# Softmax totals of a causal attention: four steps of probabilities instead of two summed before one product with ones

## The reference, cut to what matters

```
scores = jnp.einsum('bhqd,bhkd->bhqk', q, k) / jnp.sqrt(hd)
scores = jnp.where(causal, scores, -inf)
attn = jax.nn.softmax(scores, axis=-1)
y = jnp.einsum('bhqk,bhkd->bhqd', attn, v)
```

## Time and profile before

| | us |
|---|---|
| median of three runs | 2745.73 |
| lowest and highest | 2738.48, 2749.93 |
| the profiled execution | 2743.38 |
| its span on the core | 2741.5 |
| PE busy | 2482.9 |
| DVE busy | 1624.8 |
| POOL busy | 1320.2 |
| ACT busy | 1056.7 |

### The profile page before, as it was taken

The page is one execution under the profiler, slowest core; times in us unless marked ns, Lnnn a source line. Parts: engine busy times, 40 slices in busy tenths (PEclk is TensorE's granted clock), DMA queues, the critical chain, the costliest instruction groups (busy, mean ns, idle before and its releaser), DMA issues. The chain is left out here.

```text
span 2741.5 us, 40031 instructions
## 1 busy us (share of the span) xinstructions
PE 2482.9 (91%) x13407; PEld 1621.5 (59%) x13407; DVE 1624.8 (59%) x3253; ACT 1056.7 (39%) x1885; POOL 1320.2 (48%) x827
## 2 busy tenths in 40 slices
PE   6789999998758999999999999999779875999997
PEld 4667677777534444444444444444258764888885
DVE  5544555110458777777777777777136554767666
ACT  3521001111331555555555555555411111444443
POOL 3452442000432767676767676667624453333332
PEclk8999999999886999999999999999989987999998
DMA  7356655312743515151515151511186755878875
GB/s 263 108 155 198 176 168 170 95 39 61 262 134 80 133 39 133 37 134 37 135 37 136 36 134 38 121 47 48 31 274 215 168 117 179 304 280 302 296 283 195
DMA packets 231902, 397.20 MB, mean 145 GB/s; under 512 B 44540, under 2 KB 95292, under 8 KB 231620
## 3 DMA queue, kind: packets, MB, share of 16 engines
q1 hardware_dynamic: 204340, 319.62, 40.2%
q0 software_dynamic: 17152, 50.38, 5.3%
q10 hardware_dynamic: 10256, 25.21, 2.9%
HBM read 299.22 MB, written 103.76 MB: 147 GB/s over the span
## 5 line engine op out<-in xcount | busy, mean ns | idle before, releaser
L1184 ACT ACTIVATE t_prob<-t_scores_psum 128x512 f32<-128x512 f32 (+3 forms) x1280 | 610.5, 538 | 440.0 <-PE t_scores_psum L1076 241.8
L1306 POOL TENSOR_TENSOR t_two<-t_prob 128x1024 f32<-128x1024 f32 (+1 forms) x321 | 687.8, 2165 | 164.7 <-ACT t_prob L1184 110.9
L1212 DVE TENSOR_REDUCE t_part<-t_seen_psum 128x1 f32<-128x512 f32 x768 | 479.2, 682 | 141.0 <-PE t_seen_psum L1049 137.0
L1049 PE MATMUL t_seen_psum<-t_k_stack,t_q_stack 97*128 97x512 f32 (+3 forms) x1283 | 522.0, 419 | 39.6 <-DVE t_q_stack L1200 22.5
L1072 PE MATMUL t_scores_psum<-t_q_stack,t_k_stack 98*128 98x512 f32 (+3 forms) x1280 | 502.8, 404 | 5.3 <-ACT t_prob L1184 3.9
L1072 PEld LDWEIGHTS t_scores_psum<-t_q_stack,t_k_stack 98*128 98x128 f32 x1280 | 241.9, 190 | 301.5 <-ACT t_prob L1184 165.5
L1049 PEld LDWEIGHTS t_seen_psum<-t_k_stack,t_q_stack 97*128 97x128 f32 x1283 | 256.8, 201 | 90.8 <-DVE t_part L1212 36.8
L1218 DVE CUSTOM_DVE_ANT_0 t_seen_psum<-t_seen_psum,t_causal 128x128 f32<-128x128 f32 (+3 forms) x515 | 250.6, 504 | 100.9 <-PE t_seen_psum L1049 89.8
L1090 PE MATMUL t_y_acc_psum<-t_prob,t_v 128*32 128x512 f32 (+3 forms) x2576 | 301.4, 540 | 0.0
L1591 PE MATMUL z_acc_psum<-z_e_hi,z_x_hi 128*128 128x512 f32 x576 | 228.1, 396 | 0.0
L1593 PE MATMUL z_acc_psum<-z_e_hi,z_x_lo 128*128 128x512 f32 x576 | 224.9, 390 | 0.0
(11 more groups left out here) (234 smaller groups left out, 3892.7 us busy)
## 6 DMA issues: line engine op xcount, KB each, us to landing
z_raw<-in_expert_w SPq DMA_DIRECT2D x80, 512.0 KB, 6.8
z_spare<-in_expert_w SPq DMA_DIRECT2D x72, 512.0 KB, 7.1
f_w_raw<-in_wmod SPq DMA_DIRECT2D x8, 2048.0 KB, 10.1
t_q_stack<-scratch_q_hi SPq DMA_DIRECT2D x64, 256.0 KB, 5.1
t_k_stack<-scratch_k_hi SPq DMA_DIRECT2D x64, 256.0 KB, 5.0
f_w_raw<-in_w_attn SPq DMA_DIRECT2D x24, 512.0 KB, 7.0
t_inverse<-scratch_inverse SPq DMA_DIRECT2D x132, 64.0 KB, 2.0
t_y<-scratch_a_y SPq DMA_DIRECT2D x33, 256.0 KB, 4.5
```

The source lines that it names most:

```text
L1049: nc.tensor.matmul(seen[:, n % BANKS, 0:width], q_stack[par][0:SEEN, h, t0:t0 + P], k_stack[par][0:SEEN, h, c * CH:c * CH + width], start= ...
L1184: nc.scalar.activation(prob[:, step % RING, h, c0:CH], scores[:, score_bank(step, h), c0:CH], ACT.Exp, scale=1.0 / math.sqrt(D)).then_inc( ...
L1212: nc.vector.tensor_reduce(dst, seen[:, n % BANKS], AX.X, ALU.max).then_inc(seen_free, 1)
L1306: nc.gpsimd.tensor_tensor(two[:, pair % 2, heads, c0:CH], a, b, ALU.add).then_inc(two_ready, 1)
```

## The change

The sum in `two` takes four steps instead of two, and there is one totals product per quad, always over 512 columns. GpSimd makes five adds per quad: steps 0 and 1 in two halves (`add_two`), step 2 onto the sum in two halves and step 3 onto the sum for the second pair of heads (`add_more`). The first pair of heads of step 3 is added by VectorE (`add_third`), at the head of `finish` in the next step that is a multiple of four. Each add onto the sum waits for the one before it. Of the two clearings of `prob` in a diagonal quad one is left; the others aren't needed, since the later steps are added only from their first column on. The ring of four steps and the two buffers of `two` stay.

```diff
-    PAIRS = STEPS // 2
+    QUADS = STEPS // 4
     RING = 4
+    ADDS = 5
...
-            def add_up(i, pair):
+            def add_up(i, quad):
 
-                wi, kt = steps[2 * pair]
-                c0 = first_column(2 * pair)
-                pe.wait_ge(two_ready, (i * PAIRS + pair) * 2 + 6)
+                wi, kt = steps[4 * quad]
+                n = i * QUADS + quad
+                pe.wait_ge(two_ready, (n + 2) * ADDS)
+                pe.wait_ge(third_ready, n + 2)
                 if kt == 0:
                     pe.wait_ge(total_free, i * W + wi + 1)
                 for h in range(HG):
-                    last = nc.tensor.matmul(total[h * D:(h + 1) * D, c0:CH], ones[:, :], two[:, pair % 2, h, c0:CH],
-                                            start=(kt == 0), stop=(kt == steps_of(UNITS[wi][1]) - 2))
+                    last = nc.tensor.matmul(total[h * D:(h + 1) * D, :], ones[:, :], two[:, quad % 2, h, :],
+                                            start=(kt == 0), stop=(kt == steps_of(UNITS[wi][1]) - 4))
...
-                if step % 2 == 1:
-                    add_up(i, (step - TOTAL_LAG - 1) // 2)
+                if step % 4 == TOTAL_LAG - 1:
+                    add_up(i, (step - TOTAL_LAG) // 4)
...
-                    if step % 2 == 0:
-                        act.wait_ge(two_ready, (i * PAIRS + step // 2) * 2 + 2)
+                    if step % 4 != 1:
+                        act.wait_ge(two_ready, (i * QUADS + step // 4) * ADDS + {0: 2, 2: 4, 3: 5}[step % 4])
+                    if step % 4 == 3:
+                        act.wait_ge(third_ready, i * QUADS + step // 4 + 1)
...
+            def add_third(i, quad):
+
+                n = i * QUADS + quad
+                c0 = first_column(4 * quad + 3)
+                dve.wait_ge(two_ready, (n + 1) * ADDS + 3)
+                dve.wait_ge(exp_done, (i * STEPS + 4 * quad + 3) * HG + HALF + BANKS)
+                at = two[:, quad % 2, 0:HALF, c0:CH]
+                nc.vector.tensor_tensor(at, at, prob[:, (4 * quad + 3) % RING, 0:HALF, c0:CH], ALU.add).then_inc(third_ready, 1)
+
             def finish(i, step):
+                if step % 4 == 0 and 0 < i * STEPS + step <= STEPS * (G // 2):
+                    add_third(i, step // 4 - 1)
...
-            def add_two(i, pair, half):
+            def add_two(i, quad, half):
...
-                    pool.wait_ge(exp_done, (i * STEPS + 2 * pair + 1) * HG + HG + BANKS)
-                    pool.wait_ge(total_done, i * PAIRS + pair + 1)
+                    pool.wait_ge(exp_done, (i * STEPS + 4 * quad + 1) * HG + HG + BANKS)
+                    pool.wait_ge(total_done, n)
...
+            def add_more(i, quad, x, half):
+
+                n = i * QUADS + quad
+                c0 = first_column(4 * quad + x)
+                heads = slice(half * HALF, (half + 1) * HALF)
+                pool.wait_ge(exp_done, (i * STEPS + 4 * quad + x) * HG + (half + 1) * HALF + BANKS)
+                pool.wait_ge(two_ready, (n + 1) * ADDS + 2 * (x - 1) + (half if x == 2 else 0))
+                at = two[:, quad % 2, heads, c0:CH]
+                nc.gpsimd.tensor_tensor(at, at, prob[:, (4 * quad + x) % RING, heads, c0:CH], ALU.add).then_inc(two_ready, 1)
...
             def finish(i, step):
-                if step % 2 == 0:
-                    add_two(i, step // 2 - 1, 1)
+                if step % 4 == 2:
+                    add_two(i, step // 4, 1)
+                if step % 4 == 3:
+                    add_more(i, step // 4, 2, 0)
+                    add_more(i, step // 4, 2, 1)
+                if step % 4 == 0 and (i > 0 or step > 0):
+                    add_more(i, step // 4 - 1, 3, 1)
                 for wi in ended(i, step, SPLIT_LAG):
                     split(i, wi)
```

More of the change, by code:

```diff
@@ L1165, in take_total @@
             def take_total(i, wi):
-                act.wait_ge(total_done, i * PAIRS + last_step(wi) // 2 + 3)
+                act.wait_ge(total_done, i * QUADS + (last_step(wi) + 1) // 4 + 1)
                 act.wait_ge(tall_loaded, (i * W + wi + 2) * 16)
@@ L1195, in _ @@
             dve.sem_inc(tall_loaded, 16)
+            dve.sem_inc(third_ready, 1)
             dve.sem_inc(y_done, RING - Y_LAG)
@@ L1283, in _ @@
             pool.sem_inc(y_lo_done, 1)
-            pool.sem_inc(two_ready, 3)
+            pool.sem_inc(two_ready, ADDS)
             for b in range(2):
@@ L1290, in _ @@
             pool.wait_ge(sums_set, 2)
-            def add_two(i, pair, half):
-                c0 = first_column(2 * pair)
+            def add_two(i, quad, half):
+                n = i * QUADS + quad
+                c1 = first_column(4 * quad + 1)
                 heads = slice(half * HALF, (half + 1) * HALF)
                 if half == 0:
-                    pool.wait_ge(exp_done, (i * STEPS + 2 * pair + 1) * HG + HG + BANKS)
-                    pool.wait_ge(total_done, i * PAIRS + pair + 1)
-                    c1 = first_column(2 * pair + 1)
-                    if c1 > c0:
+                    pool.wait_ge(exp_done, (i * STEPS + 4 * quad + 1) * HG + HG + BANKS)
+                    pool.wait_ge(total_done, n)
+                    if c1 > 0:
                         pool.sem_inc(marks, 1)
-                        nc.gpsimd.memset(prob[:, (2 * pair + 1) % RING, :, c0:c1], 0.0).then_inc(cleared, 1)
-                        pool.wait_ge(cleared, (i * W + steps[2 * pair][0]) * (TPC // 2) + (c0 > 0) + 1)
-                a, b = (prob[:, (2 * pair + x) % RING, heads, c0:CH] for x in range(2))
-                nc.gpsimd.tensor_tensor(two[:, pair % 2, heads, c0:CH], a, b, ALU.add).then_inc(two_ready, 1)
+                        nc.gpsimd.memset(prob[:, (4 * quad + 1) % RING, :, 0:c1], 0.0).then_inc(cleared, 1)
+                        pool.wait_ge(cleared, i * W + steps[4 * quad][0] + 1)
+                a, b = (prob[:, (4 * quad + x) % RING, heads, :] for x in range(2))
+                nc.gpsimd.tensor_tensor(two[:, quad % 2, heads, :], a, b, ALU.add).then_inc(two_ready, 1)
+            def add_more(i, quad, x, half):
+                n = i * QUADS + quad
+                c0 = first_column(4 * quad + x)
[4 more added lines that the diff above has]
+                nc.gpsimd.tensor_tensor(at, at, prob[:, (4 * quad + x) % RING, heads, c0:CH], ALU.add).then_inc(two_ready, 1)
             def split(i, wi):
@@ L1324, in _ @@
                     finish(i, step)
-                    if step % 2 == 1:
-                        add_two(i, step // 2, 0)
+                    if step % 4 == 1:
+                        add_two(i, step // 4, 0)
             for step in range(SPLIT_LAG + 1):
                 if step == 0:
-                    add_two(G // 2, -1, 1)
+                    add_more(G // 2, -1, 3, 1)
                 for wi in ended(G // 2, step, SPLIT_LAG):
```

2 lines of the change are left out of this document (1 added, 1 removed).

## The result

| | before | after |
|---|---|---|
| median of four runs, us | 2743.69 | 2851.19 |
| lowest and highest | 2738.48, 2749.93 | 2844.11, 2853.0 |
| ratio and its 95% interval | | 1.0381 [1.0365, 1.0397] |
| span of the profiled execution | 2741.5 | 2849.5 |
| attention, first to last start of an exponential | 875.9 to 1967.8: 1092 | 877.0 to 2076.0: 1199 |

A forecast was written before the change was run, and what follows sets the result against it. TensorE was taken to set the pace, with VectorE chained to it; -64 (products) + 52 (new adds) + 46 (divisions) - 5 = +29 made 2743.4 into 2772, so 2775 for the median, own range 2760 to 2820.

The forecast's parts named there:

- Its signs: VectorE adds 2 to 3 us, division instructions 2 us and more, 160 totals records, TensorE idle before sees over 15 us per pass.
- The rival in which removed products give nothing: TensorE has room because weight loads fill 130.29 of 275.00 us: 2746; 0.03 of the no-change case's 0.15.
- Sum. -64 + 52 + 46 - 5 = +29: Products removed, new VectorE adds, divisions, and stalls not arising in the last 19 steps: 2743.4 becomes 2772.
- products removed: Totals products in attention go from 160 to 80: 48 x 0.97 + 32 x 0.55 = 64 us less.
- stops of TensorE, adds and divisions: VectorE held by GpSimd's adds stops TensorE: 52 us at new adds, 46 at divisions, less about 5.
- What a hold costs TensorE: Step pricing VectorE holds behind the second see: 1.8 us free with a totals product in the step, about 0.9 without.
- Divisions in full quads: Between GpSimd's unbroken adds: qc 1 held 4.4 us, 21 us in all; qc 2 and 3 held 3.6, 21 in all.
- about 0.9: Microseconds of a VectorE hold that cost TensorE nothing in a step without a totals product: 1.8 - 0.97.
- Divisions in diagonal quads: Eight divisions beside GpSimd adds of 1.29 us only: 0.5 us each, 4 us.
- Everything else ... All 0.: ScalarE's new waits (some 3 us in hand), TensorE's wait for the sum, removed memsets, SP's reciprocal wait and row loads: 0.
- Its own range is 2760 to 2820, from thirds of the two stall sums less or more: Range around the 2775 forecast, from varying the stall sums of new adds (52) and divisions (46).
- slower by more: Rival: every VectorE add just misses its boundary, -64 + 125 + 104, over 2850; beyond 2820 has 0.07 of the slower 0.55.

The follow-up runs named there:

- products_only_store_8: products_only with STORE_LAG 8 instead of 9, so stores of y go one step earlier; attention 1056.8 us (before: 1092.0).
- before_hold_5: Kernel before plus five unused one-input VectorE reductions behind each full quad, no product removed; attention 1229.6 us, whole 2885.7.
- products_only: Changed kernel without VectorE's add and with GpSimd adding only steps 0 and 1 of each quad; attention 1078.5 us, whole 2766.1.

## Why the prediction was right in sign and wrong in size

**Right: what bounds and what stalls.** The forecast was slower, with chance 0.55, by VectorE being shut out by GpSimd and holding TensorE. Its signs came: adds of 1.91 us (2 to 3 forecast; just short of it), a second instruction of a division of 2.25 (the first stayed at 1.37), 160 totals records per pass (632 seen of 640), and stops of TensorE that VectorE ended of 19 us a pass (77.4 / 4), above the 15 forecast. Exclusion was the mechanism: 65 of the add's 68 us go once a reduction of one SBUF tile stands in its place. The rival in which removed products give nothing would have made it 2746; the products were worth 44, so the earlier trace rows was the better witness.

**Wrong: "Sum. -64 + 52 + 46 - 5 = +29".** The time came out 76 above the forecast and outside the range. Term by term:

| term | forecast | measured |
|---|---|---|
| products removed | -64 | -44 (products_only_store_8) |
| stops of TensorE, adds and divisions | +93 | +68 (idle 18.2 to 85.9) |
| clock | none | +78 (3.4 to 81.9) |
| together | +29 | +102 of 107 |

- *The step that failed is the clock.* "What a hold costs TensorE" priced a stop at its own length. The profile of before has a clock of 1.00 through nearly all of attention and the earlier trace rows show no fall, so none of the rows used priced it; but a kernel whose granted clock is 1.00 while its TensorE hardly stops has that much to lose, and no bound was kept for it. before_hold_5 shows it by itself. The trace of before did hold one case, the longest stop in its attention, and the stretch behind it:

```profile
1744.19 0.50 PE L1049 MATMUL t_seen_psum<-t_k_stack,t_q_stack 97*128 97x512 f32 x1 [1.97 <-DVE t_part L1212]
```

```profile
1744.60:1751.40 6.80, 6.80 (x29) 3.83 (x31) 4.84 (x9) 2.99 (x5) 4.04 (x4) 0.50 0.81 139
```

1.97 us of stop, then 6.8 us at the half clock, 3.4 lost: priced by this row, a stop costs more than twice its length. (Its next longest, 1.44 us, is followed by no fall.)
- *Products: -64 was too much by 20.* The cadence in the earlier trace rows was a full quad's. With only the products gone and the stores earlier, a full quad inside a qc 3 unit went from 13.4 to 12.6 us and the diagonal one behind it lost 0.87, near the 0.97 of a product. But first quads of qc 1 and qc 3 units and the qc 0 unit's only quad stayed within 0.1 us. In those, other work (the reading out of totals and y at a unit's start is the one I take it for; that was not tested) sets the length.
- *Holds: size right in the main, allowance too small.* Divisions in full quads were forecast to hold VectorE 4.4 and 3.6 us and took 3.9 and 4.1 on average from start to end. But "about 0.9" free without a totals product in the step was wrong: it is 1.8 there too, on average (before_hold_5). That goes the way from 93 to 68; how much of it, and what the rest is, was not separated. The error here and the one on products nearly cancel: 68 - 44 is 24, against 29. That the sum without the clock came out so near is luck.
- *Divisions in diagonal quads: far too small.* They were priced at 0.5 us each, 4 in all, for adds of half width. The division followed above, at 1214.58, is one of these eight. Behind each of them TensorE stopped, for 1.5 to 2.1 us and 13.7 in all, and behind seven the clock fell, for 68 us in all, which took 34.
- *"Everything else ... All 0."* ScalarE's cover against GpSimd held (9.1 us of waits in after's largest group of exponentials). That of the adapter's load did not hold where TensorE gets faster: the load stays where SP's queue puts it. It took 22 us of the products' gain in products_only (VectorE waits 32.7 us for it there, 11.3 before). In after VectorE waits 9.6 us for it, no more than before.
- *The range of the sum itself.* "Its own range is 2760 to 2820, from thirds of the two stall sums less or more" does not follow: a third of 93 is 31, which gives about 2744 to 2806 around 2775.

The rival "slower by more" (over 2850) had the right region by the wrong cause: it wanted holds at their far end, 229 us of stops, and they came to 68.

## What to carry to other kernels

Where the granted clock reads 1.00 and TensorE is 98% busy, price every new stop of TensorE of a microsecond or two at about twice its length: on average the slower clock that followed was as dear as the stop itself. Before giving VectorE a sum of two SBUF tiles, look at what GpSimd does at that moment: a reduction of the same tile cost 3 us in all, the sum 68. And when work is taken off the bounding engine, look for transfers whose issue is tied to a queue and not to that engine: what then arrives relatively late gives the gain back.
